# A fused four-layer kernel: the order of TensorE's rows in a state step, who computes the D term, and when the softplus parts run

## The reference

```
xz = x @ W_in.T ; x_main, z = split(xz)         # 256 + 256 channels
x_main = silu(conv1d(x_main, width 3) + conv_b)
dbc = x_main @ W_x.T                            # 64 dt columns, 16 B, 16 C
dt  = softplus(dbc[:64] @ W_dt.T + b_dt)
for each of the 16 states n, along time t:
    h = exp(dt * A[n]) * h + dt * B[n] * x_main
    y += h * C[n]
y = (y + x_main * D_param) * silu(z)
out = layernorm(y @ W_out.T + x) * gamma + beta
# experts: 8 of hidden width 512, the two best of each token are weighted
```

## Time and profile before

| | us |
|---|---|
| median of 3 runs | 1602.43 |
| lowest to highest | 1601.49 to 1605.38 |
| profiled execution, its own time | 1599.87 |
| span of the profiled execution | 1596.9 |
| first to last `scan` of layer 2 start | 893.6 to 1331.0 |

### The profile page before, as it was taken

One profiled execution on the slowest core, in us unless ns is written; L12 is line 12 of the kernel. 1 busy time (PEld: TensorE's weight loads), 2 busy tenths in 40 slices (PEclk: granted clock), 3 DMA queues, 4 the chain that ended last, 5 costly groups with the idle time before them and its releaser, 6 DMA issues. The chain is left out here.

```text
span 1596.9 us, 21351 instructions
## 1 busy us (share of the span) xinstructions
PE 1243.1 (78%) x7092; PEld 834.7 (52%) x7092; DVE 1031.2 (65%) x2384; ACT 736.3 (46%) x1557; POOL 617.0 (39%) x609
## 2 busy tenths in 40 slices
PE   0799999998997776365677687887787774989995
PEld 0345565564464566254554455545545553766664
DVE  1266767668787444356653888988888997634444
ACT  0345555545544335133333667657557572343332
POOL 1243344344338722323311433633633543225551
PEclk9999999999999778577777798999999997699998
DMA  7300000000000112430000000000000000001113
GB/s 168 91 0 2 1 1 1 1 1 1 1 1 27 47 54 85 133 112 21 14 1 11 0 1 1 1 0 1 1 1 1 0 1 0 27 14 36 37 34 91
DMA packets 54457, 40.73 MB, mean 26 GB/s; under 512 B 13191, under 2 KB 46701, under 8 KB 54349
## 3 DMA queue, kind: packets, MB, share of 16 engines
q1 hardware_dynamic: 35660, 24.30, 5.2%
q0 software_dynamic: 4544, 9.32, 2.1%
q10 hardware_dynamic: 14146, 5.75, 1.7%
HBM read 26.32 MB, written 13.04 MB: 25 GB/s over the span
## 5 line engine op out<-in xcount | busy, mean ns | idle before, releaser
L762 POOL TENSOR_TENSOR PR<-PR,R 128x256 f32<-128x256 f32 (+3 forms) x128 | 161.1, 1259 | 269.8 <-DVE R L1216 265.1
L1693 POOL TENSOR_TENSOR YY<-YY,H 128x512 f32<-128x512 f32 x128 | 163.2, 1296 | 244.2 <-DVE H L2050 243.6
L2042 DVE TENSOR_TENSOR_SCAN H<-DA,H 128x1024 f32<-128x1024 f32 x64 | 159.4, 2490 | 0.2
L415 PE MATMUL banks<-BCR,SEL 96*128 96x512 f32 x128 | 89.2, 698 | 88.4 <-DVE H L2050 77.2
L1033 ACT ACTIVATE PR<-banks,NM 128x129 f32<-128x129 f32 (+3 forms) x256 | 132.7, 527 | 44.5 <-DVE NM L1193 43.6
L415 PE MATMUL banks<-XT,we 128*128 128x512 f32 x256 | 139.9, 667 | 11.9 <-ACT HH L1903 11.9
L415 PEld LDWEIGHTS banks<-we,HH 128*128 128x128 f32 x1024 | 131.9, 201 | 20.8 <-issue 17.7
L415 PE MATMUL banks<-we,HH 128*128 128x128 f32 x1024 | 130.9, 283 | 0.0
L1903 ACT ACTIVATE HH<-banks,be1f 128x512 f32<-128x512 f32 x128 | 84.3, 686 | 94.9 <-PE banks L415 94.1
L415 PEld LDWEIGHTS banks<-PTS,V 128*64 128x64 f32 x1280 | 72.7, 143 | 98.7 <-issue 89.1
L415 PE MATMUL banks<-PTS,V 128*64 128x128 f32 x1280 | 104.9, 295 | 15.9 <-DVE PTS L1201 9.7
(11 more groups left out here) (531 smaller groups left out, 2579.0 us busy)
## 6 DMA issues: line engine op xcount, KB each, us to landing
xsort<-zrow SPq DMA_DIRECT2D x1, 3072.0 KB, 13.1
XS<-xsort SPq DMA_DIRECT2D x12, 256.0 KB, 2.8
ysort<-PTS SPq DMA_DIRECT2D x12, 256.0 KB, 2.2
pj_stage<-in_L_ffn_w_proj SPq DMA_DIRECT2D x1, 2048.0 KB, 10.0
we<-in_L_ffn_we SPq DMA_DIRECT2D x1, 2048.0 KB, 10.8
we<-yrows SPq DMA_DIRECT2D x8, 256.0 KB, 5.0
X<-in_L_attn_resid_pre ACTq DMA_DIRECT2D x4, 256.0 KB, 4.6
xrows<-XN SPq DMA_DIRECT2D x4, 256.0 KB, 2.3
```

Source lines behind the costliest of these rows:

```text
L415: return nc.tensor.matmul(o, l, r, start=start, stop=stop)
L762: nc.gpsimd.tensor_tensor(p, p, R[:, n, :].unsqueeze(2).to_broadcast([P, 2, w]), ALU.mult).then_inc(pn, 1)
L1693: nc.gpsimd.tensor_tensor(YY[:, m, :], YY[:, m, :], H[:, k % 4, m, :], ALU.add).then_inc(ya, 1)
L2042: nc.vector.tensor_tensor_scan(h, DA[:, k % 4, :, :].rearrange("p m s -> p (m s)"), h, 0.0, ALU.mult, ALU.add).then_inc(scn, 1)
```

## The change

Six edits, all in layer 2.

1. TensorE: a step begins with `c_row(k)`, then come `chunk(2k)`, `b_row(k + 3)`, `chunk(2k + 1)`, the first spare product, the two `hidden` and the other spare products. Before it was both chunks, `c_row(k)`, spare, `hidden`, spare, `b_row(k + 3)`.
2. The D term moves from GpSimd to ScalarE: `begin_y(b)` writes `YY` with two activations. For block 0 it comes behind `dt_log(0)`, for the others behind `gate(b - 1)` at n = 1. A new semaphore `yi` tells GpSimd that a half is there, and `x_silu` waits on `yi` where it waited for `add_y` of n = 0.
3. ScalarE: `dt_log` moves from n = 10 to n = 12, behind that step's `decays`.
4. VectorE: `correction` moves from n = 10 to n = 11.
5. VectorE: `dt_sums` moves from n = 11 to n = 12.
6. VectorE: `out_stats` (n = 3) is written behind `biases` and `add_expert`, which run in other steps only (n = 2, and even n).

```diff
 def add_y(k):                                  # GpSimd
     b, n = divmod(k, NS)
-    if n == 0:
-        g.wait_ge(m0, read("c", b, 1))
-        if b:
-            g.wait_ge(yz, b)
     for m in range(2):
         if n == 0:
-            plink(nc.gpsimd.tensor_scalar(YY[:, m, :], XM[:, m, :], Dp[:, m:m + 1], None, ALU.mult))
+            g.wait_ge(yi, 2 * b + m + 1)
         else:
             g.wait_ge(ya, 2 * k + m - 1)
...
 for k in range(NK):                            # TensorE
-    for i in range(2):
-        chunk(2 * k + i)
     if k:
         c_row(k)
+    chunk(2 * k)
+    if k + 3 < NK:
+        b_row(k + 3)
+    chunk(2 * k + 1)
     for key in spare_at[k][:1]:
         spare(key)
...
-    if k + 3 < NK:
-        b_row(k + 3)
...
 def x_silu(b, m):                              # ScalarE
-        act.wait_ge(ya, 2 * NS * (b - 1) + 2)
+        act.wait_ge(yi, 2 * b)
...
+def begin_y(b):
+    if b:
+        act.wait_ge(yz, b)
+    act.wait_ge(m0, read("c", b, 1))
+    for m in range(2):
+        nc.scalar.activation(YY[:, m, :], XM[:, m, :], ACT.Copy, scale=Dp[:, m:m + 1]).then_inc(yi, 1)
...
 dt_log(0)
+begin_y(0)
 decays(0)
...
 if n == 1 and b:
     gate(b - 1)
+    begin_y(b)
...
 if n == 10 and more:
     dt_exp(b + 1)
+if n == 12 and more:
     dt_log(b + 1)
...
-if n == 10 and more:                           # VectorE
+if n == 11 and more:
     correction(b + 1)
-if n == 11 and more:
     share(b + 1)
+if n == 12 and more:
     dt_sums(b + 1)
```

More of the change, by code:

```diff
@@ L1591, in layer2 @@
             bcr, bp, cp = lsem("a2_bc_split"), lsem("a2_b_rows"), lsem("a2_c_rows")
-            bm, ex, scn, hc, ya = (lsem(f"a2_{k}") for k in ("inputs", "decays", "scans", "outs", "y"))
+            bm, ex, scn, hc, ya, yi = (lsem(f"a2_{k}") for k in ("inputs", "decays", "scans", "outs", "y", "y_begun"))
             yz, gs, var2, rs2, xo2, xo = (lsem(f"a2_{k}") for k in (
@@ L2122, in _ @@
                                 inputs(k + 2)
-                            if n == 3 and b:
-                                out_stats(b - 1)
                             if n == 2:
@@ L2128, in _ @@
                                 add_expert(k // 2 - 1)
+                            if n == 3 and b:
+                                out_stats(b - 1)
                             if n == 2 and more:
```

## The result

The changed kernel takes 1625.12 us (median of 4 runs, 1623.79 to 1626.06); the kernel before took 1603.77 on the same chip (4 runs). The ratio is 1.0134, with a 95% interval of 1.0116 to 1.0151: 21.4 us slower. Forecast were 1621, 18.6 us more.

A forecast was written before the change was run, and what follows sets the result against it. VectorE's stream was taken to set layer 2's end. Terms of -7.5 (softplus chain), +16.2 (D term), -2.1 (scans), +7.5 (W_out) and +4.5 (logits) make +18.6 us on 1599.87: 1618.5, as median 1621; range 1608 to 1634.

The forecast's parts named there:

- n = 1, 2: D term, less the scan's stretch: Blocks 1 to 3: inputs waits for later D term sums, +16.2 us; scans no longer stretched, -2.1 us.
- n = 3: product with W_out: out_stats waits longer as chunk, row, chunk precede its product: 2.5 us each, +7.5 us (0 to 12).
- n = 6: logits: choose loses its 0.74 us to spare and waits for later logits: 1.5 us each, +4.5 us (0 to 9).
- n = 7 to 13: chain and softplus: Three blocks: chain 2.0 us longer, 4.5 us of VectorE work done before correction; net -7.5 us.
- The same delay met three times: Two VectorE waits for B rows and one for the exp, between 936.95 and 968.92, are one delay.
- The chain: From the end of outs(6) through convolutions, dt products and exp to correction: 32.0 us becomes 34.0, still deciding.
- The D term: n = 1 and 2, blocks 1 to 3: behind gate on ScalarE it delays GpSimd's sums and inputs, +16.2 us.
- -2.1 us for the stretched scans: Scan beside GpSimd's tensor_scalar falls from 2.99 to 2.28 us: 3 x 0.7 gained, or nothing.
- Logits and W_out: n = 6 and n = 3: two products VectorE awaits at once come later, +4.5 and +7.5 us.
- The full-clock rival: TensorE's new order keeps lower-clock stretches away, so no change: about 0 us, 1602; chance 9%.
- -13.5: Softplus chain at n = 6 to 13: lower bound in us, if the chain isn't longer.
- Table loads: ScalarE, dt_log at n = 12: loads cost 1.28 us without drain, so it comes about level with dt_sums' second half.

The follow-up runs named there:

- e1: Kernel before with TensorE's new order alone (C row first, B row between the two chunks): 1.0192 of before, +31.2 us.
- e2: Kernel before with the D term alone moved to ScalarE, behind gate at n = 1: 1.0071 of before, +10.6 us.
- e4: Changed kernel with the D term moved between the second and third silu of n = 1, in ScalarE's gap: 1.0087 of before, +11.9 us.
- e6: Changed kernel with the D term back on GpSimd: 1.0082 of before, +13.4 us.
- e8: Changed kernel with unread filler matmuls ahead of c_row at n = 1, 6 and 7: 1.0050 of before, +7.2 us.
- e5: Kernel before with B row behind first spare product, softplus parts a step later, D term in ScalarE's gap at n = 1: 0.9863 of before, -21.0 us.
- e7: Kernel before with B row behind first spare product, softplus parts a step later, D term still on GpSimd: 0.9891 of before, -18.1 us.

## Why the prediction was right, step by step

It was right in sign and size, and nearly all the places were as told. The size owes something to luck: the four terms missed by -1.2, -2.6, +2.7 and +3.0 us, and these largely cancel. The terms, against what the starts of the scans give:

| term | forecast | measured | blocks |
|---|---|---|---|
| n = 1, 2: D term, less the scan's stretch | +14.1 | +12.9 | 6.45, 3.2, 3.2 |
| n = 3: product with W_out | +7.5 | +4.9 | 2.0, 0.8, 2.1 |
| n = 6: logits | +4.5 | +7.2 | 1.3, 2.95, 2.95 |
| n = 7 to 13: chain and softplus | -7.5 | -4.5 | -2.5, -1.1, -0.9 |

That sums to +20.5; 0.4 are in block 0, where GpSimd's sums now meet scan 2 (3.16 for 2.60), and the rest is rounding.

- *The same delay met three times.* Shown. The B row's wait went, and c_row, dbc and the exp took it over; in e1, where nothing else changed, they took 29.9 (exp), 7.3 and 6.9 us.
- *The chain.* 34.0 us forecast for block 0, 33.9 measured, the waits of 2.5 for `c_row(8)` and 2.3 at `split` came out at 3.65 and 2.42 in block 0. A second wait for a C row, at n = 11 (1.0 to 2.0 us a block), was not told. The term was still mis-sized: I took the 32.0 us of block 0 for all three blocks. In blocks 1 and 2 it had been 1087.44 - 1057.28 = 30.2 and 30.1 before, since TensorE kept its full clock in the dt part, and it is 33.6 and 33.7 now. So two blocks won 1 us and not 2.5.
- *The D term.* Shown by e2 (9.5 us of wait by itself) and e4 (none in the gap). `inputs` waited 8.84, 5.6 and 5.6 us, where 6 to 8 were told. From the start of `gate` to `inputs` are 1024.91 - 1020.99 = 3.92 us, forecast 3.95, and in block 1 `gate` came 9.37 - 6.64 = 2.73 us later behind the C row, forecast 2.7. So the step there is 6.45 us longer, for 6.5 forecast before the stretch of the scan was taken off. Two things were wrong. The -2.1 us for the stretched scans earned nothing: VectorE waits at `inputs` behind that scan in both kernels, so a scan 0.7 us shorter makes the wait 0.7 us longer (1.68 + 6.45 + 0.71 = 8.84). And in blocks 2 and 3 `gate` came 6.14 us behind the C row, 0.3 and 0.4 later and not 2.0, because `hidden` ran at the full clock there (1.98 us for four records, 3.68 and 3.58 before): +3.2 each and not 4.9. That `biases` waits for `gate` too was missed; in the changed kernel that wait lay hidden under the D term's, and it appeared in e1 and e4.
- *Logits and W_out.* Both waits came as told. The lower clock fell more on the first and less on the second than I had spread it. For W_out the forecast reasoned that TensorE, blocked at n = 2, might come to n = 3 at the lower clock; the rows beside e6 show the reverse, a short pause and chunks of 1.05 us. e8 shows the full-clock price, 1.23 forecast as 1.3.
- *The full-clock rival.* e8 made it in part: the change would still have cost about 9 us in the layer (11.7 less the filler's 2.8) with most of the low stretches gone, so "no change" was too kind. Its -13.5 needed chains no longer than before, and they were 32.3 us in blocks 1 and 2 against 30.2 and 30.1. Its sum also used 8.5, 4.5 and 3 us where the lower bounds that it names are 9.5, 0 and 0; with those it comes to -6 and not to 0.
- *Table loads.* In the changed kernel ScalarE's ln came when the row said, with 1.28 us for a load and nothing behind:

```profile
980.40 1.28 ACT L1878 ACT_TABLE_LOAD   x1
...
981.69 1.06 ACT L1878 ACTIVATE EW<-EW 128x1024 f32<-128x1024 f32 x1
```

`dt_sums` waited 0.94 a block, against "about level". The drain that the Trainium skill's page ScalarE: Activation LUTs (What ACT_TABLE_LOAD costs) puts there does not show.

## What to carry to other kernels

In a stream that waits for the slowest engine once a step, work ahead of that wait is free as long as it fits into the wait, and work behind it is not if someone needs its result at once: moving the wait to the front of the step put 2 us in front of every product that others need at once. Before a wait is removed, follow what the waiting engine meets next; here three waits were one chain, and only shortening the chain, or doing a step's other work before its end, won anything. Work given to an idle engine goes where its stream is idle, not where it reads well: the same two activations cost 10 us behind `gate` (e2), and three activations earlier they saved 3 to 5 us beside the D term on GpSimd (e5 and e7), or 1 us with TensorE's new order (e4 and e6).

## What the runs showed of the hardware

- Matmuls whose result nobody reads made a kernel faster: 24 of them, most in gaps that had been 2.4 to 4.1 us long, took 9.4 us off the layer, because chunks behind the gap took 1.05 and not 1.87 to 1.91 us. From 1056 to 1080 in the changed kernel the granted clock was 0.86; in the same steps with filler, 1048 to 1072, it was 1.00. That fits the Trainium skill, TensorE: Matmul & The Clock Gate, What's actually happening, by which the throttled state is the default and activity releases it.
- A scan takes 2.28 us by itself and up to 3.24 when GpSimd's sum of two SBUF tiles runs at its start (in the kernel before, 3.16 at 1292.99, beside two sums from 1291.49 to 1294.00, and 2.28 at 1299.41 beside none), while `inputs` and `outs`, which read one operand from PSUM, keep their 1.21 and 0.67 us beside the same sums.
- The last part of the kernel, which no edit touched, took between 265.9 and 273.3 us in the profiled executions. A difference of the spans of two single profiles would have been off by 4 us here.
